# A planner's table of durations in a graph and expert kernel: other engines hear of a tensor step later, and three steps cost what they were measured at

## The reference

```python
def _rgcn_layer(X, W, root, bias, gamma, beta, src, dst, etype, inv_deg):
    h = jnp.einsum('ni,rio->rno', X, W)
    msg = h[etype, src] * inv_deg[:, None]
    agg = jax.ops.segment_sum(msg, dst, num_segments=X.shape[0])
    out = agg + X @ root + bias
    mu = jnp.mean(out, axis=-1, keepdims=True)
    var = jnp.mean(jnp.square(out - mu), axis=-1, keepdims=True)
    out = (out - mu) * jax.lax.rsqrt(var + EPS) * gamma + beta
    out = jax.nn.elu(out)
    return out + X
...
x = x + _L0_gnn_ref(_layernorm(x, axis=-1), ...)          # 4 such layers
x = x + _L0_ffn_ref(_layernorm(x, axis=-1)[None], ...)[0]  # top 2 of 8 experts
```

## Time and profile before

| | us |
|---|---|
| median of 3 runs | 2293.65 (2291.12 to 2296.48) |
| span of the profiled execution | 2581.8 |
| TensorE busy in it | 2075.7 (80%) |
| VectorE busy | 1572.2 (61%) |
| GpSimd busy | 1253.4 (49%) |
| ScalarE busy | 818.3 (32%) |
| mean granted TensorE clock | 0.924 |

### The profile page before, as it was taken

How to read it: one execution, slowest core, us unless ns; L and a number is a source line. 1 busy time by engine, 2 the same in 40 slices (tenths; PEclk the granted TensorE clock), 3 DMA queues, 4 the chain that set the end, 5 groups by cost and what they waited for, 6 DMA issues and landing times. The chain is left out here.

```text
span 2581.8 us, 46238 instructions
## 1 busy us (share of the span) xinstructions
PE 2075.7 (80%) x16327; PEld 1296.1 (50%) x16327; DVE 1572.2 (61%) x4475; ACT 818.3 (32%) x1674; POOL 1253.4 (49%) x1223
## 2 busy tenths in 40 slices
PE   0576788787879889898889888898987988774992
PEld 0334455454545455555545545454554645454992
DVE  5976677575656356566553656566364766575665
ACT  1564556454456011111111212111011111123992
POOL 2124333544430266666716666662665656752441
PEclk9988899988889899899989999999997999986996
DMA  5698333444432487666637867765775655532335
GB/s 144 187 273 256 115 112 115 133 123 125 122 112 98 145 256 233 219 210 210 187 113 249 257 210 240 236 218 158 230 231 165 181 163 169 179 101 64 95 94 178
DMA packets 211755, 445.56 MB, mean 173 GB/s; under 512 B 40819, under 2 KB 137088, under 8 KB 209733
## 3 DMA queue, kind: packets, MB, share of 16 engines
q1 hardware_dynamic: 138357, 274.65, 34.6%
q0 software_dynamic: 61408, 156.79, 20.1%
q10 hardware_dynamic: 11760, 11.08, 1.7%
HBM read 338.14 MB, written 103.90 MB: 171 GB/s over the span
## 5 line engine op out<-in xcount | busy, mean ns | idle before, releaser
L1421 POOL DMA_INDIRECT n_BIG<-n_xd,n_SIDX x1080 | 1110.9, 1029 | 1091.2 <-PE n_PS L1907 501.3
L1888 PE MATMUL n_PS<-n_BIG 125*128 125x500 f16 x4800 | 1196.8, 388 | 69.3 <-issue 45.3
L1888 PEld LDWEIGHTS n_PS<-n_BIG 125*128 125x128 f16 x4800 | 441.1, 100 | 508.7 <-issue 142.0
L1907 PEld LDWEIGHTS n_PS<-n_OW,n_BIG 128*128 128x128 f16 x4320 | 256.3, 99 | 204.6 <-issue 68.9
L1907 PE MATMUL n_PS<-n_OW,n_BIG 128*128 128x84 f16 (+21 forms) x4320 | 303.5, 201 | 51.5 <-issue 41.6
L1927 PE MATMUL n_PS<-n_BIG,n_tabs 128*128 128x256 f16 x2400 | 299.3, 280 | 19.4 <-issue 18.9
L1601 DVE TENSOR_TENSOR n_ST<-n_PS,n_INVB 128x500 f32<-128x500 f32 x200 | 199.9, 1041 | 158.4 <-issue 47.6
L1927 PEld LDWEIGHTS n_PS<-n_BIG,n_tabs 128*128 128x128 f16 x2400 | 239.7, 101 | 62.9 <-issue 29.0
L1627 DVE SCALAR_TENSOR_TENSOR n_U<-n_PS,n_cw,n_BI 125x256 f32<-125x256 f32 x100 | 48.2, 482 | 334.9 <-PE n_PS L1927 161.3
L1296 ACT ACTIVATE n_BIG<-n_PS 128x500 f16<-128x500 f32 x300 | 164.3, 578 | 195.5 <-PE n_PS L1859 93.6
L1312 ACT ACTIVATE n_tabs<-n_ST 128x1000 f16<-128x1000 f32 x100 | 103.8, 1038 | 358.8 <-DVE n_ST L1601 192.3
(11 more groups left out here) (271 smaller groups left out, 2252.9 us busy)
## 6 DMA issues: line engine op xcount, KB each, us to landing
n_BIG<-n_a SPq DMA_DIRECT2D x175, 625.0 KB
n_a<-n_BIG SPq DMA_DIRECT2D x12, 3125.0 KB
n_xg<-n_tabs SPq DMA_DIRECT2D x53, 481.9 KB
n_INVB<-n_ind SPq DMA_DIRECT2D x100, 250.0 KB
n_BIG<-n_xd,n_SIDX POOLq DMA_INDIRECT x1080
n_BIG<-in_L_ffn_W_dram SPq DMA_DIRECT2D x32, 512.0 KB
n_xd<-n_BIG SPq DMA_DIRECT2D x75, 112.0 KB
n_whl<-n_BIG SPq DMA_DIRECT2D x16, 512.0 KB
```

What stands on the lines that cost most here:

```text
L1421: e.indirect_dma_start(m.GR[:, g % GS, :], None, m.XD[l % 2][:, :], bass.IndirectOffsetOnAxis(ap=m.SIDX[:, i:i + 1], axis=0)).then_inc(s[f ...
L1888: ins = e.matmul(m.bank(2 * p + h, 0, W), m.xps[l % 2][0:TN, part, D * k + 128 * h:D * k + 128 * h + 128], m.RA[0:TN, c.slot_of(n), W * (k ...
L1907: ins = e.matmul(m.bank(2 * p + h, at, c.width[q]), m.GR[:, g % GS, D * part + 128 * h:D * part + 128 * h + 128], ow, start=(first == 0 an ...
```

## The change

`heard(l)` is new: the time at which another engine is taken to know that the tensor step just placed is done. It is 0.3 us after TensorE's time in layer 0 and 2.8 us after it in layers 1 to 3. Four steps use it: the turn's copy on ScalarE, `post`, `fin` and the gather. Three steps get other costs: the copy 0.6 in place of 0.4, `fin` 2.0 in place of 1.5, the gather 1.3 + 9.0 in place of 1.4 + 10.0. The second program's register loads are written otherwise.

```diff
+        def heard(l):
+
+            return time["pe"] + (2.8 if l else 0.3)
...
-                turned[n] = run("act", 0.4) + 0.1
+                turned[n] = run("act", 0.6, heard(l)) + 0.1
...
                 time["pe"] += 3.4
-                later(time["pe"] + 0.3, "post", l, n)
+                later(heard(l), "post", l, n)
...
-            at = run("dve", 1.5, max(time["pe"] + 0.4, loaded[t] if l == 0 else 0.0))
+            at = run("dve", 2.0, max(heard(l), loaded[t] if l == 0 else 0.0))
...
-                    rows[q] = run("pool", 1.4) + 10.0
+                    rows[q] = run("pool", 1.3, heard(l)) + 9.0
...
-            if i % BATCH == 0:
-                n = min(BATCH, GPT - i)
-                e.reg_load(regs[0:n], m.egrow[0:1, GPT * t + i:GPT * t + i + n])
-            e.wait_ge(s["slot_free"], e.snap(regs[i % BATCH], min_val=1, max_val=c.P) + S8)
+            at = GPT * t + i
+            e.wait_ge(s["slot_free"], e.value_load(m.egrow[0:1, at:at + 1], min_val=1, max_val=c.P) + S8)
...
-                e.wait_ge(s["evac"], e.snap(regs[last], min_val=1, max_val=c.G + 1))
+                e.wait_ge(s["evac"], e.value_load(m.tabrow[0:1, last:last + 1], min_val=1, max_val=c.G + 1))
```

More of the change, by code:

```diff
@@ L2657, in dense_scalar @@
     e.wait_ge(s["prep"], c.prep["gp_sub"])
-    regs = [e.alloc_register(f"er{TD}_{i}") for i in range(BATCH)]
     for t in range(TD):
@@ L3092, in dense_tensor @@
     e.wait_ge(s["prep"], c.prep["b1t"])
-    regs = [e.alloc_register(f"pr{TD}_{i}") for i in range(3 * BATCH)]
+    regs = [e.alloc_register(f"pr{TD}_{i}") for i in range(2 * BATCH)]
     n_os = 0
@@ L3096, in dense_tensor @@
         n = min(BATCH, c.P - p0)
-        for w in range(3):
+        for w in range(2):
             at = w * c.PT * 128 + p0
@@ L3107, in dense_tensor @@
                 e.wait_ge(s["os"], n_os) if n_os else None
-                last = 2 * BATCH + min(i + 1, n - 1)
-                e.wait_ge(s["evac"], e.snap(regs[last], min_val=1, max_val=c.G + 1))
+                last = 2 * c.PT * 128 + p0 + min(i + 1, n - 1)
+                e.wait_ge(s["evac"], e.value_load(m.tabrow[0:1, last:last + 1], min_val=1, max_val=c.G + 1))
             e.matmul(m.PS[:, bass.ds(clear, 2)], m.OS[:, p % S8, :], m.Z[:, :], start=True, stop=False,
```

## The result

| | us | ratio, 95% interval |
|---|---|---|
| kernel before, median of 4 runs | 2292.39 (2288.69 to 2296.48) | |
| kernel changed, median of 4 runs | 2318.82 (2315.55 to 2320.85) | 1.0118 [1.0097, 1.0139] |

Slower by 26 us, where 13 faster was forecast. Sign and size were wrong, and the time lies outside the forecast's range.

A forecast was written before the change was run, and what follows sets the result against it. TensorE, busy 2075.7 of 2581.8 us, was taken as the bound, with only its idle time and slow clock movable. Terms -18 - 16 + 13 + 6 = -15 us, scaled by 0.888 to -13, gave 2280 us, range 2256 to 2310.

The forecast's parts named there:

- Part 1: Layers 1 to 3: TensorE's waits at turns and products, 69.3 us in the trace, shrink to give minus 18 us.
- fast end: Count of missing tensor work between dependent steps with shortest delays: turn and product in layers 1 to 3, 18.7 to 20.3.
- Part 2: Layers 1 to 3: a new tile's first step no longer waits for its pair (n_XT), minus 16 us.
- Part 3: Ends of layers 1 to 3: layers end in chunks alone, waiting for rows at GpSimd's period, plus 13 us.
- 34 us that I named as decisive: TensorE idle in the last 25 us of layers 1 to 3 together, above which the forecast's balance would be wrong.
- The clock, left out of the sum: Five products in the chunk runs of layers 1 and 2 might cost 2.8 more each, 14 us, at slower clock.
- rival B: Ends of layers 1 to 3: chunk runs become the bound, GpSimd late and clock falling, +21 us, 2312 us; chance 0.22.
- Part 4: Layer 0, where only the costs differ: short turns and products grow, plus 6 us.
- Part 5: Layer boundaries, experts, end of routing and the untaken second program: no further effect, 0 us.
- A: No net effect: turn and product at the fast end, layer 0 unchanged, 2294 us; chance 0.16.
- C: VectorE is freed more than counted: minus 45, scaled minus 40, 2254 us; chance 0.10.
- D: The second program's longer code reaches into the first by instruction loading: 2294 us; chance 0.02.

The follow-up runs named there:

- e11: Kernel before with 10.3 in place of 10.0 for a gathered row in layer 0 alone: 2289.28 us, ratio 0.9975.
- e8: The change in layers 1 to 3 alone, layer 0 in its old order, against the kernel before: 2315.67 us, ratio 1.0088.
- e12: Kernel before with only the gather's line new (1.3 + 9.0, heard) in layers 1 to 3: 2296.49 us, ratio 0.9998.
- e13: Kernel before with turn, fin and post new in layers 1 to 3, the gather's line old: 2317.19 us, ratio 1.0090.
- e14: Kernel before with turn, fin and post new in layers 1 to 3, gather there 1.3 + 9.0 without heard: 2428.40 us, ratio 1.0563.
- e17: Kernel before with only fin and post heard late in layers 1 to 3, fin costing 2.0: 2346.15 us, ratio 1.0218.
- e9: The change in layer 0 alone, layers 1 to 3 with old numbers, against the kernel before: 2306.05 us, ratio 1.0047.
- e15: Order of before with the second program's loads as changed, traced on a quick chip, against the kernel before: 2299.90 us, ratio 1.0008.
- e3: Kernel before with only the second program's register loads written as in the change: 2588.71 us, ratio 1.0006.
- e7: Order of before with the second program's loads as changed, on a slow chip, against the kernel before: 2617.77 us, ratio 1.0026.
- e6: The change with the old costs but heard in all four places, slow chip, against the kernel before: 2590.63 us, ratio 0.9912.
- e10: Kernel before with heard in all four places in layers 1 to 3, old costs, quick chip: 2327.03 us, ratio 1.0132.

## Why the prediction was wrong

**The basis.** The step that failed first stands in the prediction's first part: "Waits at a turn (L1772) are 24.6 + 7.8 and at a product (L1923) 21.5 + 15.4, together 69.3 us." 46.1 of these were put down to "issue" in the earlier trace rows, and the quick chip has 24.4 in all, a third. Two signs stood in front of me: the word "issue", and a profiled span 288 us above the runs. I scaled by 0.888, as if every wait shrank alike. They did not. Place by place (both traces have the same sequence), the boundaries keep their 21.3 us; of the nameless 46.1, 16.0 stand at 17 steps where the quick chip has no gap, and 30.1 at 9 steps where it has 11.1; the named 23.2 have 11.8 there. So a name did not tell what would stay: the pair's named 9.0 us at chunks are gone, and its nameless ones at dense steps are partly there (9.6 against 2.4). And the waits for rows, 23.3 on the quick chip, were not in the trace that I had at all.

**Part 1, turn and product, forecast -18, measured +1.9** (-0.4 without the last product). My own count from the orders had the answer as its fast end: 18.7 before and 20.3 after, against 24.4 and 26.3 measured. I placed the kernel at 0.51 between the ends because the trace's 69.3 stood there. At the fast end the step gives plus 1.6. The repeats leave the sign open: without the last product, e11 has 28.2 and e8 16.7. VectorE's wait before `post` fell by 126 us on the quick chip, as the 100 or more that I asked for, but TensorE's steps did not wait for VectorE often enough for it to matter.

**Part 2, the pair, forecast -16, measured -2.7.** The waits on n_XT vanished, as predicted, in the result's trace; e8 has one of 2.9 left. The fast end said 2.0 before and 0 after, and 2.7 were there. Mechanism right, size wrong for the same reason.

**Part 3, runs of chunks, forecast +13.** Near in size, and that is partly luck: the idle time in the last 25 us rose by 13.1, to 22.4 us, within the 15 to 25 given and under the 34 that I named as decisive. But layer 3, where I had 8.7 against nothing, has 8.5 against 8.8: before's order waits for rows there already, and between the last gathers GpSimd issues the routing's own indirect DMAs (L1436), which my count of 7.7 us left out. And in layer 2 the run stands for `fl` and not for rows. The waits for rows did rise by 12.1 over the three layers, about half of it in these runs. The cause was misplaced too: the gather's later hearing brings none of it (e12), the chain's does (e13). Wrong in reach as well: the runs e14 and e17 show losses of 130 and 49 us without such ends. I looked at where the chunks fall behind at the end and not at how both kinds of steps are spread over the layer.

**The clock, left out of the sum.** I priced the slow products of rival B at 14 us and dropped them since a rule pointed the other way. Measured: 7 us more busy time in layers 1 to 3 (6 in e8). The product at 1589.48, behind 5.56 us without work, is the predicted case. By the rule of the Trainium skill ("TensorE: Matmul & The Clock Gate", what is actually happening) the throttled state is the default and activity releases it; the trace agrees at this place, and it shows no filled waits elsewhere that pay for it, because the waits to be filled were not there.

**Part 4, layer 0, forecast +6.** In these two traces 628 against 627; the timed e9 says 11, and e8 with the old layer 0 says 20 for the rest, 31 together against 26. The reason that I gave is not borne out: the waits at turn and product of this layer, which were to grow by some 5 us, are 28.8 before (e15) and 26.9 after. A number of this layer that is moved by 0.3 gives minus 6. Where the size is right, it is luck.

**Part 5.** Boundaries -2.3 us against 0. Second program: nothing (e3, e7, e15), as said.

**The sum again, with quick numbers**, layers 1 to 3: turn and product +1.9, pair -2.7, boundaries -2.3, rows +12.1, the routing's copy and small ones +0.8, together 9.8 of waits, which is the 10 by which the idle time grew; clock +7. That is 17 of the 26 us; the profiled spans differ by 16. The other 10 lie between the profiled executions and the medians and in layer 0, and I can't part them.

**The rivals.** A had the right place (turn and product at the fast end) for a wrong reason: profiling does not make this kernel longer, since e15's profiled execution took 2299.34 us beside a median of 2299.90. Its sum was wrong too, since it kept the pair's -9. C needed more to free than there was. D is answered by e3. B named the right place and outcome, 2312 us, with a condition (34 us) that wasn't met. The cause was B's in part, waits for rows and slow products, at a smaller size, mostly outside the ends, and with nothing on the other side.

## What to carry to other kernels

Compare the profiled execution's span with the timed runs before taking a wait from it. In the later rounds the span lies within 21 us of the median of its kernel on the same chip; in the trace of the prediction it was 288 us above the runs. From such a trace take no wait, with a named releaser or without, but take a second trace first: here 69.3 us became 24.4, and 23.3 us of another kind came up.

Counting the tensor work between dependent steps of the list gave the right answer at its fast end; where a count and a trace disagree by more than a factor of three, ask on which chip the trace was taken.

Numbers in a planner work as a set: two entries moved as the change has them cost 2%, the set 1%, and another single entry nothing. Try each alone and together, in the layers where it acts.

## What the runs showed of the hardware

The same instructions in the same order take 2297 us on one chip and 2597 on another (spans of e15 and e7). Layers 1 to 3 have 73 us idle against 208 and 1192 us of busy TensorE against 1265, layer 0 takes 627 us against 716, and the granted clock is 0.945 against 0.915. But the last stretch, from the routing's last L1798 on through the experts, takes 226 us and 228, with TensorE busy 165 and 166 and a clock of 0.87 on both. So the two differ in the graph layers and not in the experts; what sets these apart is not shown. An order can gain 0.9% on one kind of chip (e6) and, with the same TensorE sequence in layers 1 to 3, lose 1.3% on the other (e10). What makes the gaps is open: the profile names no releaser.

Idle time that is scattered over these layers comes with slower matmuls. Against e15, the traces have 10 us more idle and 7 more busy (the change), 17 and 6 (e8), 14 and 17 (e10), 21 and 17 (e17), 96 and 44 (e14), at a lower granted clock in every layer.
